# Expert routing counted inside attention, rows scattered into one DRAM region per expert, and results scatter-added into the output

## What is computed

```
h   = LN(x)                                   # no gain; then LN again with gain and bias
att = softmax(q k^T) v @ Wo + (silu(gate) * hid) @ Wff2   # 16 heads of 64; q from h, k and v from context; ff width 1024
x   = x + tanh(g_xattn) * att
m   = LN(x)
shared = silu(m @ sh_up + b) @ sh_down + b    # one expert that all tokens use
scores = softmax(m @ gate_w.T)                # 8 experts
w, i   = top_k(scores, 2); w = w / (sum(w) + 1e-20)
y      = sum over the two chosen experts e of w_e * (silu(m @ up[e] + up_b[e]) @ down[e] + down_b[e])
x   = x + tanh(g_ffn) * (y + shared)
```

## Time and profile before

| | us |
|---|---|
| median of 3 runs | 632.21 (631.11 to 632.3) |
| span of the profiled execution, first to last instruction | 629.7 |
| TensorE busy in it | 550.9 |
| VectorE / ScalarE / GpSimd busy | 447.8 / 343.6 / 237.9 |

### The profile page before, as it was taken

How to read it: one execution, slowest core, us unless ns; L and a number is a source line. 1 busy time by engine, 2 the same in 40 slices (tenths; PEclk the granted TensorE clock), 3 DMA queues, 4 the chain that set the end, 5 groups by cost and what they waited for, 6 DMA issues and landing times.

```text
span 629.7 us, 13343 instructions
## 1 busy us (share of the span) xinstructions
PE 550.9 (87%) x4099; PEld 522.0 (83%) x4100; DVE 447.8 (71%) x1176; ACT 343.6 (55%) x1108; POOL 237.9 (38%) x254
## 2 busy tenths in 40 slices
PE   1779999999999999999999999998477999995175
PEld 1778999999999999999999999987477999984175
DVE  7767878778778878778877876768997445551057
ACT  2467656756666756665766665776603444531042
POOL 3355523323323333332342342354626444127600
PEclk9989999999999999999999999999859999997568
DMA  4550200100100100000100000005202333323303
GB/s 144 164 179 30 84 2 1 36 0 0 33 0 0 33 0 0 33 0 0 33 0 0 0 17 1 2 18 168 69 18 83 119 117 115 86 75 102 108 1 133
DMA packets 26691, 31.54 MB, mean 50 GB/s; under 512 B 2947, under 2 KB 24388, under 8 KB 26660
## 3 DMA queue, kind: packets, MB, share of 16 engines
q1 hardware_dynamic: 23244, 22.88, 11.2%
q0 software_dynamic: 3088, 8.27, 4.8%
q10 hardware_dynamic: 330, 0.02, 0.0%
HBM read 22.61 MB, written 8.55 MB: 49 GB/s over the span
## 4 chain that ended last, share of the span: by engine, by line
PE 68%; DVE 15%; ACT 5%; issue 5%; another core or an unknown queue 5%; DMA 0%; DVEq 0%; POOL 0%; ACTq 0%; SPq 0%
PE bank L1325 21%; PE bank L1326 19%; PE bank L1327 19%; PE bank L1459 4%; PE bank L1522 2%; DVE xn L847 2%; ACT pr L647 1%; PE bank L1653 1%; PE bank L1645 1%; DVE acts L1018 1%; ACT acts L622 1%; DVE xs L1301 1%; ACT weights L695 1%; DVE q_t L1086 1%
## 5 line engine op out<-in xcount | busy, mean ns | idle before, releaser
L507 POOL TENSOR_TENSOR pr<-pr,rden 128x512 f32<-128x512 f32 x64 | 66.7, 1042 | 161.2 <-DVE rden L1013 161.0
L1325 PE MATMUL bank<-acts,weights 128*128 128x256 f32 x384 | 110.6, 288 | 5.8 <-DVE weights L895 2.9
L1327 PE MATMUL bank<-acts,weights 128*128 128x256 f32 x384 | 109.8, 286 | 0.0
L1326 PE MATMUL bank<-acts,weights 128*128 128x256 f32 x384 | 109.6, 286 | 0.0
L647 ACT ACTIVATE pr<-bank,nmax 128x128 f32<-128x128 f32 x256 | 90.4, 365 | 28.1 <-DVE nmax L984 27.1
L1325 PEld LDWEIGHTS bank<-acts,weights 128*128 128x128 f32 x384 | 74.8, 195 | 10.2 <-issue 4.0
L1325 PE MATMUL bank<-weights,acts 128*128 128x256 f32 x256 | 80.5, 314 | 2.1 <-POOL acts L512 2.0
L512 POOL TENSOR_TENSOR acts<-uf,acts 128x256 fp32r<-128x256 f32 x64 | 47.1, 736 | 83.1 <-ACT acts L639 83.1
L1326 PEld LDWEIGHTS bank<-acts,weights 128*128 128x128 f32 x384 | 74.5, 194 | 2.4
L955 DVE TENSOR_TENSOR acts<-bank,acts 64x256 fp32r<-64x256 f32 x128 | 53.9, 421 | 30.1 <-ACT acts L622 29.3
L1327 PEld LDWEIGHTS bank<-acts,weights 128*128 128x128 f32 x384 | 74.5, 194 | 0.0
(11 more groups left out here) (248 smaller groups left out, 1630.6 us busy)
## 6 DMA issues: line engine op xcount, KB each, us to landing
slot_rows<-stage SPq DMA_DIRECT2D x35, 128.0 KB
ct<-in_ctx SPq DMA_DIRECT2D x8, 256.0 KB, 2.7
xs<-in_x SPq DMA_DIRECT2D x8, 256.0 KB, 4.8
spare<-in_L_xattn_Wff SPq DMA_DIRECT2D x8, 256.0 KB, 4.4
norm_rows<-xn SPq DMA_DIRECT2D x7, 256.0 KB, 2.2
out_x<-xs SPq DMA_DIRECT2D x3, 512.0 KB, 3.0
stage<-in_L_xattn_Wff SPq DMA_DIRECT2D x2, 512.0 KB, 4.4
stage<-in_L_xattn_Wo SPq DMA_DIRECT2D x2, 512.0 KB, 5.0
```

What stands on the lines that cost most here:

```text
L507: pool.tensor_tensor(pr[:, s % 2], pr[:, s % 2], rden[:, s % 2, :].unsqueeze(2).broadcast_to((P, 4, P)), ALU.mult).then_inc(probs_ready, 1)
L1325: pe.matmul(ps, wts[1], mov[0], start=first, stop=False, skip_group_check=True)
L1326: pe.matmul(ps, wts[0], mov[0], start=False, stop=False, skip_group_check=True)
L1327: return pe.matmul(ps, wts[0], mov[1], start=False, stop=last, skip_group_check=True)
```

## The change

**Routing moves into the attention iterations.** Logits of a group are now made in `s` 5 and transposed at once (`turn_logits`); VectorE finds the best two (`max`, `max_index`), a 0/1 table `hot`, and at the end of the iteration three small matmuls (`count_choices`) give each row's rank. A running count `taken` per expert gives the row's slot in that expert's region of `slot_rows`. GpSimd sends the rows (256 values, token number and weight: 258 words) with two indirect DMAs for the first choice at the end of the iteration and two for the second in `s` 1 of the next. The normalising steps of the layer norm are drawn together so that they end in `s` 3.

**The sort goes:** `norm_rows`, the batched top two, ranks, one-hot matrices and the token list. In its place stand `pads` (SP fills 640 rows behind each expert's count before the last groups, nine stores, 5.4 MB in all) and `tables` on VectorE, which from the eight counts makes each tile's row and expert.

**The tile loop has 39 tiles** (32 and 7) for all 16 sequences. SP loads each tile with two plain DMAs (rows; token number and weight), VectorE multiplies the result by the weight, and GpSimd adds the tile to `out` in DRAM with an indirect DMA that accumulates. The output of the shared expert with the residual is stored to `out` before. Two adds can be in flight; the first tile of an expert, and each of the tiles behind the 36 that hold rows, waits until the tile before it has landed. `out` gets 256 rows in front that take the adds of padding rows and are cut off.

**The dense last group and the way back go**: `dense_up`, `dense_down`, `add_dense`, the 28 gathers and 28 `add_back`. The fourth part of the shared expert moves ahead of the tile loop.

```diff
-MIX_MID = ["FF0", "QP2", "FF1", "FF2", "QP3", "FF3", "FF4", "FF5", "X1T", "TXc", "FF6", "GL", "FF7",
+MIX_MID = ["FF0", "QP2", "FF1", "FF2", "QP3", "FF3", "X1T", "FF4", "GL", "FF5", "TXc", "FF6", "FF7",
-NTS = NB - 2
-NCH = 2 * NTS
-TILES = NCH + NE - 1
+TILES = 2 * NB + NE - 1
+REGION = NTOK + P
+AHEAD = 2 * GT + P
...
 (SP)
+            for e in range(NE):
+                first = sp.value_load(start_at[0:1, e:e + 1], min_val=0, max_val=PAD_ROW - AHEAD)
+                sp.dma_start(slot_rows[bass.ds(first, AHEAD)].rearrange("(a p) n -> p a n", p=P),
+                             pad_row.unsqueeze(1).broadcast_to((P, AHEAD // P, ROW))).then_inc(pads_stored, 16)
...
+            def load_tile(t, slot_of):
+                row = sp.value_load(tile_row[0:1, bass.ds(t, 1)], min_val=0, max_val=PAD_ROW)
+                sp.dma_start(rows_g[:, slot_of, :], slot_rows[bass.ds(row, P), 0:D]).then_inc(gathered[slot_of], 16)
+                sp.dma_start(meta[:, bass.ds(t, 1), :].rearrange("p a n -> p (a n)"), slot_rows[bass.ds(row, P), D:ROW]
+                             ).then_inc(gathered[slot_of], 16)
...
 (GpSimd)
+            def send(rows, c, done):
+                for t in range(2):
+                    pool.indirect_dma_start(slot_rows[:, :], bass.IndirectOffsetOnAxis(ap=slot[:, 2 * t + c:2 * t + c + 1], axis=0),
+                                            rows[:, t, :], None).then_inc(done, 16)
...
+                    if s == 1 and not first:
+                        second_rows(g - 2, xrow)
...
+                    if last:
+                        pool.wait_ge(pads_stored, 16 * (NE + 1))
+                    first_rows(g - 1, xrow)
...
-            for t in range(4, TILES):
-                gather(t)
-            for t in range(NTS):
-                    pool.indirect_dma_start(back(2 * t + c), None, slot_rows[:, :],
...
+            pool.wait_ge(written, 16 * TPS)
+            for t in range(TILES):
+                pool.wait_ge(y_copied, t + 1)
+                if t >= 1:
+                    due = pool.value_load(turn[0:1, t:t + 1], min_val=16, max_val=16 * (TILES // 2 + 2))
+                    pool.wait_ge(y_added[t % 2], 16 * (t // 2) + 16)
+                    pool.wait_ge(y_added[(t - 1) % 2], due)
...
+                pool.indirect_dma_start(out_rows, bass.IndirectOffsetOnAxis(ap=meta[:, t, 0:1].bitcast(I32), axis=0),
+                                        ys[:, t % 4, :], None, compute_op=ALU.add).then_inc(y_added[t % 2], 16)
...
 (VectorE, tile loop; ys now lies in xn)
+                            dve.wait_ge(y_added[b % 2], 16 * (n // 2))
-                    dve.tensor_copy(ys[:, b, :], bank[6 + c % 2][:, 0:D]).then_inc(y_copied, 1)
+                    dve.tensor_scalar(ys[:, b, :], bank[6 + c % 2][:, 0:D], weight, None, ALU.mult).then_inc(y_copied, 1)
...
 (TensorE)
+            def count_choices(b, n):
+                pe.wait_ge(chosen_done, n + 1)
+                pe.matmul(b[:, 0:3 * NE], before, chosen, start=True, stop=False, skip_group_check=True)
+                pe.matmul(b[:, NE:3 * NE], ones, chosen[:, 0:2 * NE], start=False, stop=False, skip_group_check=True)
+                return pe.matmul(b[:, 2 * NE:3 * NE], ones, chosen[:, 0:NE], start=False, stop=True,
...
-            shared_up(3)
-            dense_up(0, 0)
...
-            for e in range(2, NE):
-                dense_up(e, e % 2)
-                dense_down(e - 1, (e - 1) % 2)
-            dense_down(NE - 1, 1)
```

960 lines of the change are left out of this document (476 added, 484 removed).

## The result

The changed kernel takes 663.72 us (median of 4 runs, 660.95 to 665.91), the kernel before 631.66 us beside it: ratio 1.0501, 95% interval 1.0455 to 1.0546. It is slower by 5%; 595 was predicted, with 573 to 621 as the range. The profiled execution has a span of 664.1 us and took 665.91.

A forecast was written before the change was run, and what follows sets the result against it. TensorE was taken to bound attention and tile loop, the sort between them, the gathers' run the end. First copy 484.3 + 5.6 = 489.9, plus 103 for the adds = 592.9, plus 2.5 = 595.4: 595 predicted, range 573 to 621.

The forecast's parts named there:

- Sum 0.8 x 7 = 5.6: Attention: seven iterations each grow by 0.54 us of TensorE work and 0.25 us of waits; 5.6 us in all.
- The 0.25 us "on that": Attention: allowance per iteration for two extra norm steps ahead of feed-forward results and TensorE's wait for the logits' copy.
- The worry that I priced highest: Attention: GpSimd's four scatters per iteration without cover, 4 x 1.25 us x 7 = 35 us; held unlikely.
- Two chains of equal length: I count nothing: Between attention and tile loop: the new routing chain, +50 us, replaces 51.4 us; counted as 0 (-4 to +8).
- The products are the same: Tile loop: TensorE's products unchanged, so 39 tiles at 2.11 us take 82 us from the first copy.
- R = 4.2: Tile loop: time from one add's issue to the next that waited for its landing; 24.5 x 4.2 = 103 us.
- The estimate of 3.6: Tile loop: the add's issue-to-next-issue time estimated from the skill, 0.95 + 2.0 + 0.6 us, giving a chain of 88 us.
- "What goes": 71.2: Behind the tile loop, from 558.5 on: dense products, gathers, adds back and last stores vanish, 71.2 us.
- rival C: Last seven tile steps or the chain behind attention: the gathers' stall of 27 us returns, giving 622; chance 0.07.
- Rival D: Attention gets thicker: VectorE busier, 2.5 us lost per iteration without cover, giving 612; chance 0.09.
- A: Tile loop: adds are hidden and TensorE stays the bound, R up to 3.5, giving 578; chance 0.17.
- B: Tile loop: adds slow enough to eat the gain, slower than before from R = 5.7, far end 644; chance 0.09.

The follow-up runs named there:

- no_route: On top of x1_later, VectorE's finding of experts, weights and slots left out for the first seven groups: 697.9 us (one run), 51.6 us per attention iteration.
- middle: Changed kernel with TensorE's work between attention and tile loop reordered, last projection first and logits ahead of the shared expert's down products; attention unchanged: 658.3 us.
- x1_later: Changed kernel with the transposes of normed rows and the logits half a unit to a unit later in each attention iteration: 650.5 us.
- send_later: Changed kernel with GpSimd's two first-choice scatters issued behind the next iteration's first unit instead of ahead of it: 663.3 us.
- spread: On top of x1_later, VectorE's layer norm steps spread as in the kernel before and the norm applied one unit later, in s 4: 658.7 us.
- bias128: Changed kernel with the bias matmuls of shared and expert products reading all 128 partitions instead of 2: 647.6 us.
- plain: Changed kernel with the accumulation left out, each tile's indirect DMA overwriting its rows of out: 659.2 us.
- att2: On top of x1_later, VectorE's steps ahead of the first probabilities and between two feed-forward results moved behind these, norm still applied in s 3: 657.1 us.
- after_again: The changed kernel, unchanged, run again: 663.4 us against 631.3 for the kernel before beside it.
- after: The changed kernel as first measured and profiled: 663.72 us, ratio 1.0501 to the kernel before.
- before: The kernel before the change, unedited: 631.66 us beside the changed kernel.
- bias_free: Changed kernel with bias matmuls over 128 partitions and adds that wait only at an expert's first tile and at empty tiles: 639.6 us.

## Why the prediction was wrong

The span was to be 592.9 and is 664.1, 71.2 us more. Term by term:

- **"Sum 0.8 x 7 = 5.6"** for attention: this is the step that failed, 34.5 of the 71.2 us. TensorE's 0.54 us is about right: it is busy for 0.1 us (no_route) to 0.6 us (middle) more per iteration where the clock doesn't fall. The 0.25 us "on that" for waits is 4.5: its idle time in six iterations went from 2.4 to 29.4 us. I counted VectorE's time as free because it had 69 us idle in 320 and did not ask when in the iteration it was free: transposes, norm and logits were moved ahead by a unit or more, to where VectorE had not got their input. That position is 1.4 us per iteration (x1_later against middle), the routing steps themselves are 1.8 (no_route), waits whose step isn't found 1.8, and 0.4 is a clock that fell behind such waits, which the prediction had nowhere. The worry that I priced highest, GpSimd's scatters, cost nothing (send_later for two of the four, spread for all).
- **"Two chains of equal length: I count nothing"**: +7.2, and the term's own steps had summed to 50 us, which is 58.5. From the end of attention the residual came at +7.4 instead of +4.7, the turned logits at +32.4 instead of +24, the slots at +41.8 instead of +35.5. bias128 gives 5.5 us of the 8.5 back (slots at +36.2): they are bias matmuls of the shared expert over 2 partitions.
- **First tile to first result**, not in the sum: +4.7. TensorE idled 10.5 us for the first loads, and its granted clock is 0.50 (1.2 GHz) from 525.58 to 536.16; this and the bias matmuls together are the 4.7, as bias128 has 6.4 us here (clock 0.75) and the kernel before 5.9 (clock 1.00).
- **"The products are the same"**: false. The rows of bias matmuls changed from 128 to 2 partitions in a line of the diff that I passed over; 0.75 us per tile. It hid behind the adds, so alone it explains 7 of their 17.5 us, and 8.6 us of the stretches ahead, which are the two terms above.
- **R = 4.2**: 4.44 alone and mostly 4.5 to 4.6 in the loop; 24.5 times 0.24 to 0.4 is 6 to 10 us. From the first add to the last one's landing (4.44 us behind its issue) are 120.5 us instead of 103. The estimate of 3.6 from the Trainium skill, "DMA: Bandwidth & Descriptors", section "Anatomy of one DMA", was low: the issue is 1.56 instead of 0.95, and its 2.0 us and one source are borne out by plain (2.21 us behind the issue), but the second source costs 0.67 us instead of 0.3.
- **Not counted**: 1.3 us from first result to first add, and 6.2 from the last landing to the end.
- **"What goes": 71.2** was right on this chip, and none of it came back; rival C's stall did not return. Rival D named the place of the largest miss with 3.3 us per iteration instead of 5.5; A and B were about R, which decided little. B's outcome, slower than before, came true for reasons that B doesn't name.

## What to carry to other kernels

Before counting an engine's idle time as room, look at when it is idle: work that is put ahead of something that the bound waits for is not hidden by idle time later in the loop. Beside the waits of two variants compare busy time and granted clock: one that waits no longer can still be slower. A long instruction on the profile's chain is a cause only if the next step had nothing else to wait for. Read every shape in a diff, a bias row too, and compare each "unchanged" product by its form. And measure a baseline on more than one chip before explaining 27 us of it.

## What the runs showed of the hardware

- A matmul over 2 or over 64 partitions between matmuls over 128 costs 0.37 us more than one over 128 (2.11 to 2.86 and 2.87 us per tile, with two of them).
- VectorE's instruction on 38 numbers in SBUF was held for 8.02 us by a run of six GpSimd instructions; it got in between none of them.
- Where TensorE waited 1.9 to 2.15 us once per iteration, its granted clock fell to 0.50 for about 3.6 us beside that wait in 6 of 6 iterations (att2), 4 (spread), 3 (after_again), 2 (after) or none (middle); where no wait was over 1.2 us (before, x1_later, no_route) it never fell.
- An indirect DMA of 128 rows of 1 KB that adds to DRAM takes 1.56 us to issue and 4.44 from issue to the next that waited for it; without the add 0.96 and 3.17. With up to four in flight GpSimd issues one per 1.86 us (bias_free).
- Beside the same run of 28 gathers three engines stand still for some 25 us on some chips and not on others (span 629.7 and 605.1 us).
